# The last expert's rows in a table of their own, and the finish in halves on VectorE

## The reference, cut to what matters

```python
y = toks + y * layer_scale[:, None, :]                 # each expert's slots
out = jnp.zeros((N, Cc), dtype=x.dtype)                # N = 4 * 1024 tokens
out = out.at[tok.reshape(-1)].add((wgt[..., None] * y).reshape(-1, Cc))
...
s = _L1_attn_ref(xn, L1_attn_Wq, L1_attn_Wk, L1_attn_Wv, L1_attn_Wg)
g = _silu(_L1_ffn_ref(xn, ...))
x = x + s * g
```

## Time and profile before

| | |
|---|---|
| median of 3 runs (lowest to highest) | 1028.86 us (1028.47 to 1029.36) |
| the profiled execution, its own time | 1039.62 us |
| its span, first to last instruction | 1037.8 us |
| PE busy | 885.6 us (85% of the span) |
| DVE busy | 823.6 us (79%) |
| ACT busy | 724.5 us (70%) |
| POOL busy | 263.8 us (25%) |
| DMA | 147.19 MB, mean 142 GB/s |

### The profile page before, as it was taken

The page is one execution under the profiler, slowest core; times in us unless marked ns, Lnnn a source line. Parts: engine busy times, 40 slices in busy tenths (PEclk is TensorE's granted clock), DMA queues, the critical chain, the costliest instruction groups (busy, mean ns, idle before and its releaser), DMA issues. The chain is left out here.

```text
span 1037.8 us, 25027 instructions
## 1 busy us (share of the span) xinstructions
PE 885.6 (85%) x9373; PEld 468.3 (45%) x9374; DVE 823.6 (79%) x1698; ACT 724.5 (70%) x1489; POOL 263.8 (25%) x246
## 2 busy tenths in 40 slices
PE   3999897999999999999898898778998998799940
PEld 3666542333333333333334676533444444377830
DVE  6665497999999999999823765579999999737875
ACT  2666316888888888888774544467999999867731
POOL 4865300000000000000003666400444442014543
PEclk9999759999999999999989888678999999989985
DMA  4679778533333453230004899693454542556716
GB/s 162 228 264 345 244 148 207 166 65 67 72 66 85 93 117 84 64 68 14 12 25 122 294 338 279 208 231 72 97 112 79 103 87 47 133 175 175 254 50 224
DMA packets 133143, 147.19 MB, mean 142 GB/s; under 512 B 19149, under 2 KB 94490, under 8 KB 132384
## 3 DMA queue, kind: packets, MB, share of 16 engines
q1 hardware_dynamic: 129696, 140.60, 49.7%
q0 software_dynamic: 3328, 4.99, 1.7%
HBM read 77.63 MB, written 69.54 MB: 142 GB/s over the span
## 5 line engine op out<-in xcount | busy, mean ns | idle before, releaser
L839 ACT ACTIVATE probsB<-psB 128x512 f32<-128x512 f32 (+2 forms) x640 | 309.9, 565 | 100.4 <-PE psB L913 78.8
L776 DVE TENSOR_REDUCE mxB<-psB 128x1 f32<-128x512 f32 (+2 forms) x448 | 259.6, 644 | 9.4 <-PE psB L884 8.6
L906 PE MATMUL psB<-q_groups,k_groups 64*128 64x512 bf16 (+3 forms) x768 | 209.1, 333 | 29.4 <-ACT probsB L839 19.5
L877 PE MATMUL psB<-k_groups,q_groups 64*128 64x512 bf16 (+3 forms) x768 | 219.8, 343 | 3.0 <-PEq L293 1.7
L944 PE MATMUL psB<-probsB,vB 128*32 128x512 f32 (+3 forms) x1536 | 166.6, 506 | 0.5 <-ACT probsB L839 0.5
L1709 ACT ACTIVATE psD<-psD 128x896 f32<-128x896 f32 (+2 forms) x192 | 153.4, 799 | 16.7 <-PE psD L1763 16.2
L906 PEld LDWEIGHTS psB<-q_groups,k_groups 64*128 64x128 bf16 x768 | 67.4, 94 | 186.4 <-ACT probsB L839 162.5
L1640 DVE TENSOR_REDUCE sumsD<-psD 128x1 f32<-128x128 f32 (+3 forms) x256 | 113.5, 483 | 13.3 <-PE psD L1786 11.3
L884 PE MATMUL psB<-hideB,chooseB 64*128 64x128 bf16 (+1 forms) x1024 | 117.3, 210 | 0.0
L776 DVE TENSOR_REDUCE mx2B<-psB 128x1 f32<-128x384 f32 (+2 forms) x192 | 105.4, 596 | 13.6 <-PE psB L884 11.8
L1763 PE MATMUL psD<-k_groups,q_groups 64*128 64x512 bf16 (+3 forms) x384 | 104.0, 343 | 12.4 <-ACT psD L1709 3.6
(11 more groups left out here) (219 smaller groups left out, 1490.9 us busy)
## 6 DMA issues: line engine op xcount, KB each, us to landing
v<-vaugA SPq DMA_DIRECT2D x4, 2048.0 KB, 8.9
vB<-v SPq DMA_DIRECT2D x16, 512.0 KB
q_groups<-q SPq DMA_DIRECT2D x32, 200.0 KB
k_groups<-k SPq DMA_DIRECT2D x32, 200.0 KB
q_groups<-q SPq DMA_DIRECT2D x32, 192.0 KB
k_groups<-k SPq DMA_DIRECT2D x32, 192.0 KB
back<-emptyB SPq DMA_DIRECT2D x16, 256.0 KB, 4.2
o<-outB SPq DMA_DIRECT2D x128, 32.0 KB, 1.9
```

The source lines that it names most:

```text
L776: nc.vector.tensor_reduce(dst, src, AX.X, ALU.max).then_inc(max_read, 1)
L839: nc.scalar.activation(probs[:, n % DEEP, 0:w], st[n % BANKS][:, 0:w], ACT.Exp, scale=DH ** -0.5).then_inc(exp_done, 1)
L877: ins = nc.tensor.matmul(bank[:, to:to + w], q[half[r], s, hq // 2, t * P:t * P + P], k[half[r], s, hq // 2, HALF * c:HALF * c + w], start ...
L906: ins = nc.tensor.matmul(bank[:, to:to + w], k[half[r], s, hq // 2, jt * P:jt * P + P], q[half[r], s, hq // 2, i0:i0 + w], start=True, sto ...
```

## The change

- A new HBM table `late` of N rows is cleared by eight more stores of 256 KB in attention, behind those of `back` and before `store(0, 0)`.
- Experts 0 to 6 scatter into `back` as before. Expert 7 scatters into `late`. Its index is that of `back`, less N where it is at least N; one more DVE instruction on 128x5 makes it.
- PE puts each tile of expert 7's `y` into a PSUM bank of its own (6, 7, 0, 1, 5) and counts each. DVE goes tile by tile: bias, scale, `z` (`last_expert`).
- SP loads `back` when the scatters of experts 0 to 6 have landed, and `late`, four loads of 512 KB, when those of expert 7 have.
- DVE's list behind expert 6 is now: `join(0)`, `join(1)`, `last_expert`, `join(2)`, `join(3)`, `gate_retention(3)`, and then a second addition for each batch (`join_late`).
- The SiLU, the product and the addition of `x1` go in halves of a batch (512 columns), all additions of `x1` on DVE and none on POOL, and the stores are eight of 256 KB.

```diff
@@ -172,7 +172,7 @@
     def wait_slots(self, engine):
-        engine.wait_ge(self.slots_cleared, 16 * (NE + 2 * NTILES // 4))
+        engine.wait_ge(self.slots_cleared, 16 * (NE + 3 * NTILES // 4))
 
...
         engine.wait_ge(self.x1_stored, 32 * B + 1)
@@ -711,6 +711,9 @@
                     sp.dma_start(A["back"][g * 4 * P:(g + 1) * 4 * P, :].rearrange("(t p) c -> p t c", p=P),
+                                 empty[:, 0:4, 0:D]).then_inc(slots_cleared, 16)
+                for g in range(NTILES // 4):
+                    sp.dma_start(A["late"][g * 4 * P:(g + 1) * 4 * P, :].rearrange("(t p) c -> p t c", p=P),
                                  empty[:, 0:4, 0:D]).then_inc(slots_cleared, 16)
...
                     if x == 1:
@@ -1861,6 +1864,7 @@
         turned_bank = ps[:, 0:2, :].rearrange("p b f -> p (b f)")
+        last_at = [ps[:, bank, 0:P] for bank in (6, 7, 0, 1, 5)]
         ident, x, fc1, fc2, b1, b2, ls = expert.ident, expert.x, expert.fc1, expert.fc2, expert.b1, expert.b2, expert.ls
...
         warm = m.sb("warmE", [P, 1])
@@ -1876,7 +1880,7 @@
         gated, x1 = m.sb("gatedE", [P, B, NT, D]), m.sb("x1E", [P, B, NT, D])
-        rows = [t[:, :, :, :].rearrange("p s a f -> p (s a f)").bitcast(F32).rearrange("p (b t c) -> p b t c", b=B, t=NT)
+        moe, prod = [t[:, :, :, :].rearrange("p s a f -> p (s a f)").bitcast(F32).rearrange("p (b t c) -> p b t c", b=B, t=NT)
                 for t in (groups.q, groups.k)]
...
 
@@ -1884,12 +1888,16 @@
         y_biased, y_scaled, shared_ready, z_ready = (m.sem(n) for n in ("y_biasedE", "y_scaledE", "shared_readyE", "z_readyE"))
-        sent = [m.sem(f"sentE{i}") for i in range(2)]
+        sent, late_sent = [m.sem(f"sentE{i}") for i in range(2)], m.sem("late_sentE")
+        late_to, late_step = m.sb("late_toE", [P, SLOT_TILES]), m.sem("late_stepE")
         summed, ret_turned, ret_read = (m.sem(n) for n in ("summedE", "ret_turnedE", "ret_readE"))
...
         rows_before = [16 * 4, 16 * 3, 16 * 2, 16 * 5 * 2]
-        moe_ready, silued, prod_ready, done, stored = (m.sem(n) for n in ("moe_readyE", "siluedE", "prod_readyE", "doneE", "storedE"))
+        late_in, late_before = [*side_in, w_in[0], w_in[1]], [16 * 5 * 2, 16 * 5 * 2, 16 * 5 * 3, 16 * 5 * 3]
+        fours = [slice(0, 4), slice(4, NT)]
+        joined, moe_ready, silued, prod_ready, done, stored = (m.sem(n) for n in (
+            "joinedE", "moe_readyE", "siluedE", "prod_readyE", "doneE", "storedE"))
         WEIGHTS, RETS, SENT, DEN_STEPS, RET_STEPS = 16 * 5, 16 * 5, 16 * SLOT_TILES, 4, 9
...
         with nc.Block() as block:
@@ -1906,7 +1914,11 @@
                         back = A["back"][kk * N + b * S:kk * N + (b + 1) * S, :]
-                        sp.dma_start(rows[kk][:, b], back.rearrange("(p t) c -> p t c", p=P)).then_inc(rows_in[b], 16)
+                        sp.dma_start((moe, prod)[kk][:, b], back.rearrange("(p t) c -> p t c", p=P)).then_inc(rows_in[b], 16)
+
+                def load_late(b):
+                    sp.wait_ge(joined, b + 1)
+                    sp.dma_start(prod[:, b], A["late"][b * S:(b + 1) * S, :].rearrange("(p t) c -> p t c", p=P)).then_inc(late_in[b], 16)
 
...
                 kept_until.wait_retention(sp)
@@ -1923,27 +1935,32 @@
                             sp.dma_start(x1[:, b], A["x1"][b].rearrange("p (t c) -> p t c", c=D)).then_inc(x1_loaded, 16)
-                for i in range(2):
-                    sp.wait_ge(sent[i], SENT * (NE // 2))
+                sp.wait_ge(sent[0], SENT * 4)
+                sp.wait_ge(sent[1], SENT * 3)
                 for b in range(B):
                     load_rows(b)
+                sp.wait_ge(late_sent, SENT)
                 for b in range(B):
-                    sp.wait_ge(done, b + 1)
-                    sp.dma_start(A["out"][b].rearrange("(t p) c -> p t c", p=P), res[:, b]).then_inc(stored, 16)
-                sp.wait_ge(stored, 16 * B)
+                    load_late(b)
+                for b in range(B):
+                    for half, t4 in enumerate(fours):
+                        sp.wait_ge(done, 2 * b + half + 1)
+                        sp.dma_start(A["out"][b, 4 * P * half:4 * P * half + 4 * P].rearrange("(t p) c -> p t c", p=P),
+                                     res[:, b, t4, :]).then_inc(stored, 16)
+                sp.wait_ge(stored, 16 * 2 * B)
 
...
             def _(pool):
-                for e in range(NE):
+                for e in range(NE - 1):
                     for t in range(SLOT_TILES):
...
                                                 oob_is_err=False).then_inc(sent[e % 2], 16)
-                pool.wait_ge(x1_loaded, 16 * B)
-                for b in range(B - 1):
-                    pool.wait_ge(prod_ready, b + 1)
-                    nc.gpsimd.tensor_tensor(res[:, b], rows[1][:, b], x1[:, b], ALU.add).then_inc(done, 1)
+                for t in range(SLOT_TILES):
+                    pool.wait_ge(z_ready, SLOT_TILES * (NE - 1) + t + 1)
+                    pool.indirect_dma_start(A["late"], bass.IndirectOffsetOnAxis(ap=to[:, 1, t:t + 1], axis=0),
+                                            z[:, 1, t, :], None, bounds_check=N - 1, oob_is_err=False).then_inc(late_sent, 16)
 
...
             def _(pe):
@@ -1987,11 +2004,13 @@
                         pe.wait_ge(y_biased, 2 * e)
+                    if e == NE - 1:
+                        pe.wait_ge(ret_read, 2 * B)
                     for t in range(SLOT_TILES):
+                        at = last_at[t] if e == NE - 1 else ps[:, 6 + t // 4, (t % 4) * P:(t % 4) * P + P]
                         for c in range(FC):
-                            ins = nc.tensor.matmul(ps[:, 6 + t // 4, (t % 4) * P:(t % 4) * P + P], hT[:, c, t * P:t * P + P],
-                                                   fc2[:, i, c, :], start=(c == 0), stop=(c == FC - 1))
-                        if t in (3, SLOT_TILES - 1):
+                            ins = nc.tensor.matmul(at, hT[:, c, t * P:t * P + P], fc2[:, i, c, :], start=(c == 0), stop=(c == FC - 1))
+                        if t in (3, SLOT_TILES - 1) or e == NE - 1:
                             ins.then_inc(y_done, 1)
...
                         turn_retention(e // 2)
@@ -2029,8 +2048,9 @@
                     if b >= 2:
-                        act.wait_ge(prod_ready, b - 1)
-                    nc.scalar.activation(gate[:, b % 2], rows[0][:, b], ACT.Silu).then_inc(silued, 1)
+                        act.wait_ge(prod_ready, 2 * b - 2)
+                    for t4 in fours:
+                        nc.scalar.activation(gate[:, b % 2, t4, :], moe[:, b, t4, :], ACT.Silu).then_inc(silued, 1)
 
...
             def _(dve):
@@ -2128,7 +2148,31 @@
 
-                for e in range(NE):
+                def last_expert():
+                    e = NE - 1
+                    i, at, first = e % BUFS, e % 2, 2 * e
+                    dve.wait_ge(w_in[i], WEIGHTS * (e // BUFS + 1))
+                    dve.wait_ge(sent[at], SENT * (e // 2))
+                    V.tensor_scalar(late_to[:, :], x[:, i, :, D + 1], float(N), -float(N), ALU.is_ge, ALU.mult).then_inc(late_step, 1)
+                    dve.wait_ge(late_step, 1)
+                    V.tensor_tensor(to[:, at, :], late_to[:, :], x[:, i, :, D + 1], ALU.add)
+                    dve.wait_ge(shared_ready, e + 1)
+                    dve.wait_ge(y_scaled, 2 * e)
+                    dve.wait_ge(z_ready, SLOT_TILES * e)
+                    for t in range(SLOT_TILES):
+                        dve.wait_ge(y_done, first + t + 1)
+                        V.tensor_tensor(y[:, t, :], last_at[t], b2[:, i, :], ALU.add).then_inc(y_biased, 1)
+                        dve.wait_ge(y_biased, first + t + 1)
+                        V.tensor_tensor(scaled[:, t, :], y[:, t, :], ls[:, i, :], ALU.mult).then_inc(y_scaled, 1)
+                        dve.wait_ge(y_scaled, first + t + 1)
+                        V.scalar_tensor_tensor(z[:, at, t, :], scaled[:, t, :], x[:, i, t, D:D + 1], shared[:, at, t, :],
+                                               ALU.mult, ALU.add).then_inc(z_ready, 1)
+
+                def join(b):
+                    dve.wait_ge(rows_in[b], rows_before[b] + 32)
+                    V.tensor_tensor(moe[:, b], moe[:, b], prod[:, b], ALU.add).then_inc(joined, 1)
+
+                for e in range(NE - 1):
                     b = e // 2
...
                         add_retention(b)
@@ -2143,25 +2187,34 @@
                         gate_retention(b)
-
-                def join(b):
-                    dve.wait_ge(rows_in[b], rows_before[b] + 32)
-                    V.tensor_tensor(rows[0][:, b], rows[0][:, b], rows[1][:, b], ALU.add).then_inc(moe_ready, 1)
+                join(0)
+                join(1)
+                last_expert()
+                join(2)
+                join(3)
+                gate_retention(B - 1)
 
                 def result(b):
-                    dve.wait_ge(silued, b + 1)
-                    dve.wait_ge(gated_ready, B)
```

(27 more changed lines are left out.)

## The result

| | median (lowest to highest) | against before, 95% interval |
|---|---|---|
| before, 4 runs | 1029.11 us (1028.47 to 1030.09) | |
| changed, 4 runs | 1041.07 us (1038.57 to 1044.55) | 1.0118 [1.0085, 1.015] |
| changed again, 6 runs, another round of before at 1024.73 us | 1035.78 us (1033.15 to 1039.31) | 1.011 [1.0079, 1.0142] |

The change makes the kernel 1.1% slower, 11 to 12 us. The profiled execution of the changed kernel has a span of 1036.8 us, 1.0 us under the one of before (1037.8), so two single spans don't show the loss. The place where the time went is found only by laying the stretches side by side.

What follows compares the result with a forecast made beforehand. Bound: SP's zero stores ahead of place(1) in attention; at the end, waits for back's rows and loads, then DVE. 7.3 + 4.1 = 11.4 us on 1028.86 gives 1040.3 us, 8-in-10 range 1033 to 1044.5.

Steps and rivals of the forecast that it cites:

- The sum: Whole kernel: 7.3 us in attention plus 4.1 at the end, 11.4 us slower, to 1040.3 us.
- The stores: Start of attention: eight more zero stores ahead of place(1) at 0.91 us each lengthen PE's wait by 7.3 us.
- a longer wait pays this once as well, so I add nothing for it: Attention: PE already runs at 1.2 GHz for 5.2 us after its wait, so no clock cost was added.
- The upper bound, 9.3 us: Start of attention: the most the eight stores were to cost, at 1.16 us each.
- VectorE held by two joins: End: DVE stands from 996.7 until join(0) at 1005.9, join(1) at 1009.4; expert 7's work queues behind, late loads at 1020.15.
- The finish: End: join_late(0) starts 3.5 us after the late loads, then DVE is the bound for 14.5 us instead of 19.65.
- the last store: End of the span: 256 KB where it was 512, taking 3.7 us for 4.1.
- Hidden stores: Attention: stores quick enough that place(1) isn't late cost 0 to 4 us; about 1033 us; chance 15%.
- Both at their upper bounds: Attention and end: 9.3 us for stores and some 6 for the end, 1044 to 1045.5 us; chance 11%.
- The overlap works: End: back's rows arrive by 997.9, DVE isn't held, end gains 8.4 us; 1027.8 us in all; chance 3%.
- Nothing in sum: Whole kernel: hidden stores and an end at its lower bound or below, within 0.2%; chance 3%.
- The 10.8 us: Whole kernel: median of the runs lies this far under the profiled execution; no view says where.

Runs made afterwards that it cites:

- experiments 1 and 5: Before plus eight unused zero stores, 1.009; changed kernel with its eight moved behind place(2) to place(9), 1.004; before plus four such stores, 1029.30 us in one run.
- the first four kernels of the experiments: Before plus eight zero stores, 1.009; changed with those moved, 1.004; changed with last_expert and gate_retention(3) before the joins, 1.0076; before with finish in halves on VectorE, 0.9962.

## Why the prediction came out right, point by point

**The sum.** Predicted +11.4 us and 1040.3; measured 1041.07, and +11.3 to +12.1 by the two ratios. The traces split it. A takes 51.1 us on average in the four traces with the stores of before at their old place and none added (49.2, 49.4, 51.6, 54.0) and 59.5 in the four with eight more (58.7 to 60.1): 8.4 us. The end takes 38.7 us on average in five traces with the old end (38.3 to 39.0) and 42.2 in three with the new one (41.9, 42.3, 42.5): 3.5 us. Together 11.9. The prediction had 7.3 and 4.1. It was 1.1 us short in the first and 0.6 us over in the second, and that the sum lies within half a microsecond of the traces is in part luck.

**The stores.** The mechanism was right: nothing hid them, and PE's wait took nearly all of them: between the same four and four traces it grows from 2.7 to 9.7 us on average, by 7.0, and the rest of A by 1.4. The wait itself was to be some 12 us and was 10.7 and 9.2, since the forecast started from the longest of the four. The eight take 7.2 to 7.6 us, so one costs 0.91 to 0.95 us in SP's list in the traces with eight, for 0.91 predicted. The Trainium skill's ceiling for the fabric (DMA: Bandwidth & Descriptors, Specifications) would have made 4.8 us of them, an estimate; no trace here shows the stores near it. The step that failed is "a longer wait pays this once as well, so I add nothing for it". It holds against the one trace the prediction had. But that trace has a wait of 4.8 us where others have 1.6, 1.7 and 2.8. In two of these four the clock doesn't fall, and there the longer wait brings the fall as a new cost of 1 to 2.7 us. The upper bound, 9.3 us, held the 8.4.

**VectorE held by two joins.** Right, and it is the heart of the end: `join(0)` started 4.88 us behind the first load (predicted 4.81), `join(1)` 7.53 (8.25; in the second trace 8.16), the first scatter 1.13 us behind the first `z`, the late loads 7.48 us behind that scatter (7.44). The edit of the order alone took 6.5 us off the end.

**The finish.** From `join_late(0)` to DVE's end 14.35 us for 14.5, from the late loads to `join_late(0)` 3.65 for 3.5. The term that was mis-sized is the last store: from DVE's end to the end of the span are 3.07 us, not 3.7 (4.1 before). A store of 256 KB landed after 2.5 us (median) where 512 KB had taken 3.2. The Trainium skill has a fit for a DMA from GpSimd (DMA: Bandwidth & Descriptors, Anatomy of one DMA), in which the bytes cost their number over 436 GB/s. As an estimate 256 KB less are 0.6 us less by it; the traces show 0.7 for SyncE's stores, where I took 0.4.

**The rivals.** *Hidden stores*: fallen by experiments 1 and 5. *Both at their upper bounds*: neither place reached its bound (8.4 for 9.3, 3.5 for 7.2). *The overlap works*: fallen; `join(1)` started 9.7 us behind expert 6's last scatter. When the order is mended, the overlap does work for the scatters, and the loads then slow each other. *Nothing in sum*: fallen.

**The 10.8 us** between the first profiled execution and the median, which the prediction left open, can be placed in part against the second trace of before (spans 1037.8 and 1021.1, 16.7 us apart): 1.6 us before `place(0)`, 2.4 in A, 7.0 from `place(2)` to the start of the experts, 5.3 in the experts, 0.4 at the end. So it is neither spread evenly nor all in one place. It isn't a cost of recording as such either: the profiled executions of the other kernels that have several runs lie between 6 us under and 2 us over their medians. The runs of before themselves lie between 1020.59 and 1035.73 us on the several chips, still under the 1039.62 of the first profiled execution; why that one was so long stays open.

## What to carry to other kernels

Work that "anybody can do any time", such as clearing a table, isn't free in a queue that runs in order: look at what stands behind it in that list, and who waits for that. Before a wait is moved ahead in an engine's list, compare the time its data can be there with the time that the work behind it is ready; here 9 us of VectorE stood in front of output that was there. And test the parts of a change one at a time: the finish in halves was worth 4 us and was buried under costs of 8.4 us in one place and, by one pair of traces, 6.5 in the other.

## What the runs showed that I had not expected

- In these traces the granted clock stayed at 1.00 with a wait of PE of 1.6 or 1.7 us. With waits of 2.8 us and more it fell to 0.5, mostly already during the wait, and PE worked at 1.2 GHz for 3.4 to 6.2 us behind it. Moving one queue of stores away takes both the wait and the fall.
- An indirect scatter that was issued among or just behind eight loads of 512 KB needs 5.3 to 5.4 us from its start until SP can go on, and 2.2 to 2.3 us with no loads pending, though the two stand in different queues.
- The experts' stage, from PE's first transpose to expert 6's last scatter, takes 84.1 to 85.5 us in eight traces and 88.1 to 89.6 in five; before itself has 89.6 in its first trace and 84.3 in its second. The five are the first trace of before and all four traces of the first four kernels of the experiments, which ran on one chip; the seven traces of the two later chips are all among the eight. So it may go with the chip; that wasn't tested. The 4 us are as large as the whole effect at the end, and a reason to compare stretches and not spans.
